# A Mamba scan whose column order is read across the rows of one input buffer

## The chip, the cores and the metric

The kernel runs on one core of a Trainium2 chip. The metric is device time in microseconds (us) of one execution of the whole program, from the first to the last instruction with a little around it; lower is better. All data are fp32.

## The reference

Eight images of 192 x 48 x 48 go through two layers. Layer 0 is a two-dimensional Mamba block (a selective scan in four directions), layer 1 an attention block with depthwise convolutions. The part that matters here is how layer 0 makes the four sequences of the scan and uses them:

```python
xx = gelu(depthwise_conv3x3(xx) + conv_b)               # (8, 384, 48, 48)
x_hw = xx.reshape(Bb, Dd, L)                            # by rows
x_wh = xx.transpose(0, 1, 3, 2).reshape(Bb, Dd, L)      # by columns
xs = jnp.stack([x_hw, x_wh, x_hw[..., ::-1], x_wh[..., ::-1]], axis=1)
x_dbl = jnp.einsum('bkdl,kcd->bkcl', xs, x_proj_w)      # x_proj: dts, B and C
dts, Bs_, Cs_ = jnp.split(x_dbl, [R, R + N], axis=2)
delta = softplus(einsum('bkrl,kdr->bkdl', dts, dt_w) + dt_b[None, :, :, None])
# per step: h = h * exp(delta * A) + (delta * u) * B ;  y = sum_n h * C
ys = selective_scan(xs, delta, A, Bs_, Cs_, Ds)         # K = 4 directions, N = 16 states
```

The four results are brought back to row order and added, then normalised, gated, projected (out_proj) and added to x.

## The kernel before

The 384 channels lie as J = 3 tiles of 128 partitions; a tile has L = 2304 positions (48 rows of 48), so one position is 4 bytes and one image row 192 bytes of a partition. A chunk is CH = 384 positions, 8 rows (or 8 columns), and a direction has NC = 6 chunks. Each of the eight images goes through four stages with a barrier of all engines after each: `front`, `scan_phase`, `back` and `attention`. Each engine runs its own program, ordered by hand, and semaphores hold them together. The convolution for the next image is done by the vector engine in the attention stage.

**The scan's input.** `u_v` holds the input twice: `u_v[:, 0]` by rows and `u_v[:, 1]` by columns. The convolution writes the row copy and ScalarE applies GELU to it in place, one channel tile at a time (L978, semaphore `gel`). The column copy is made in `front` by `column_copy`, one channel tile on each of three engines: VectorE tile 0 (L766), GpSimd tile 1 (L1206, a multiplication by one), ScalarE tile 2 (L980). Each of these reads with a stride of one image row and writes contiguously, waits for its tile's GELU, and counts up `uwh`.

**front on TensorE.** Two passes of x_proj (L463), o = 0 over the row copy after `gel` has reached 3, o = 1 over the column copy after `uwh` has reached 3. A pass has six groups, one for each chunk, of three matmuls 128x128 by 384 columns, accumulated over the channel tiles. The trace shows each fp32 matmul as two records, so a pass is 36 records and both are 72. A group goes to one of two PSUM banks of its pass; VectorE copies 64 rows of it into `stage` (L774) and ScalarE the other 64 into `dts` (L987). A bank may be filled again when both have read it. After a pass SyncE sends `stage[:, o]` to DRAM (L386), from where the rows of B and C are read back, broadcast over partitions, during the scan (L365).

**scan_phase.** Directions k = 0 to 3 one after the other, six chunks each; k even goes by rows, k odd by columns. For each chunk and each of the 16 states GpSimd multiplies `du` with a row of B (L1222), ScalarE makes exp(delta A) in PSUM (L1049), VectorE scans three times (L798), VectorE or GpSimd multiplies with C (L817 for ten states, L1232 for six), and TensorE adds the products in PSUM by an identity matmul (L490). Once a chunk:

- GpSimd makes `du` = delta times u for the next chunk (`delta_u`, L1211), between the work of states 12 and 13; the next L1222 needs it.
- ScalarE makes delta's softplus (L996 to L1007), VectorE its last step (L781), from matmuls of TensorE (L470).
- TensorE adds the y stored so far (L503, k = 1 to 3) or the skip term (L500, k = 0), and ScalarE stores y (L1031). y is kept by rows alone. So at k odd the three matmuls of L503 already read `y_v` in column order, eight columns of 48 positions with one image row (192 bytes) between neighbours, through the view `y_v.rearrange("p j (h w) -> p j w h", h=H)[..., 8 columns, :]`. At k = 2 the same line reads contiguous positions.

**Memory.** One buffer `area` is cut into parts by hand; the scan's parts lie behind `U`, one after the other.

Of the kernel before, what the change touches and what calls it, by code (L numbers as in the profile page):

```python
# [22 lines left out]
ALU = mybir.AluOpType  # L23
ACT = mybir.ActivationFunctionType
ds = bass.ds

NB, C, H, W = 8, 192, 48, 48
L = H * W
# [3 lines left out]
J = DI // 128  # L32
K, N, R = 4, 16, 12
CH = 8 * W
NC = L // CH
# [10 lines left out]


U = 0
DTS = U + 2 * J * L
DT0 = (64, 0, 96, 32)  # L50
ROWS = 4
ROWB = DTS + L
# [5 lines left out]
SCAN_END = HB + NH * JC  # L58
# [8 lines left out]
V = 0  # L67
XP2 = V + PAIRS * L
XN1 = XP2 + 3 * PADS
AREA = SCAN_END  # L70
X = AREA - CT * L
VT = X - MT * PAIRS * 128
KZ = VT - PAIRS * L
# [11 lines left out]
def build(nc, t, out):  # L85
    ctx = ExitStack()
    with ctx:
# [3 lines left out]
        def sem(name):  # L91
            return ctx.enter_context(nc.semaphore(name))
# [9 lines left out]
        d_diag = sb("d_diag", [128, J, 128])  # L102
        w_cv = sb("w_cv", [128, J, 9])
        b_cv = sb("b_cv", [128, J])
# [21 lines left out]
        ones = sb("ones", [128, 1])  # L126
# [17 lines left out]
        def ar(off, n, p0=0, p1=128):  # L144
            return area[p0:p1, off:off + n]

        u_v = ar(U, 2 * J * L).rearrange("p (o j l) -> p o j l", o=2, j=J)
        dts = ar(DTS, L)
        row_b = ar(ROWB, 2 * ROWS * CH).rearrange("p (s r l) -> p s r l", s=2, r=ROWS)
        row_c = ar(ROWC, 2 * ROWS * CH).rearrange("p (s r l) -> p s r l", s=2, r=ROWS)  # L150
# [42 lines left out]
        pad0 = sem("pad0")  # L193
        conv = sem("conv")
        gel = sem("gel")
        uwh = sem("uwh")
        xp_mm = sem("xp_mm")
        xp_ev = sem("xp_ev")
        xp_dv = sem("xp_dv")
# [63 lines left out]
        def alone(e):  # L263


            e.sem_inc(passed, 1)
# [11 lines left out]
        def wait_conv(e, b, j):  # L278

            e.wait_ge(conv, b * 54 + (18 * j + 18))  # L280
# [8 lines left out]
        def conv_taps(e, base, i, done, src, dst, w, bias):  # L289

            base = snap(e, base + 18 * i)
            acc = dst.rearrange("p (h w) -> p h w", h=H)
            for tap in range(9):
                dy, dx = divmod(tap, 3)
                for half in range(2):
                    r = H // 2 * half
                    a, x = acc[:, r:r + H // 2], src[:, r + dy:r + dy + H // 2, dx:dx + W]
                    if tap == 0:
                        e.tensor_scalar(a, x, w[:, i, 0:1], bias[:, i:i + 1], ALU.mult, ALU.add).then_inc(done, 1)  # L299
                    else:  # L300
                        e.wait_ge(done, base + (2 * tap - 1 + half))
                        e.scalar_tensor_tensor(out=a, in0=x, scalar=w[:, i, tap:tap + 1], in1=a,  # L302
                                               op0=ALU.mult, op1=ALU.add).then_inc(done, 1)
# [6 lines left out]
        def copy_vt(e, b, p, g):  # L310
# [2 lines left out]
            e.wait_ge(vt_mm, b * 10 + (5 * p + g + 1))  # L313
            e.activation(vt[:, p, 4 * g:min(4 * g + 4, MT)],
                         ps[:, 3 + g % 2, 0:n].rearrange("p (m c) -> p m c", c=128), ACT.Copy).then_inc(vt_ev, 1)

        def column_copy(e, b, j):

            wait_conv(e, b, J - 1)
            e.wait_ge(gel, b * 3 + (j + 1))  # L320
            return u_v[:, 1, j].rearrange("p (w h) -> p w h", w=W), u_v[:, 0, j].rearrange("p (h w) -> p w h", h=H)


        def walk(e, body):

# [9 lines left out]
        def pos(k, c):  # L335

            return c * CH if k < 2 else (NC - 1) * CH - c * CH
# [87 lines left out]
        def _(e):  # L425
# [27 lines left out]

            def front(b):
                for o in range(2):
                    e.wait_ge(gel if o == 0 else uwh, b * 3 + 3)
                    alone(e)
                    with e.Fori(0, 3) as cc:
                        for s in range(2):
                            e.wait_ge(xp_ev, b * 12 + cc * 2 + (6 * o + s + 1))  # L460
                            e.wait_ge(xp_dv, b * 12 + cc * 2 + (6 * o + s + 1))
                            for j in range(J):
                                m = e.matmul(ps[:, 2 * o + s, 0:CH], w_xp[:, j, o],  # L463
                                             u_v[:, o, j, ds(cc * 2 * CH + s * CH, CH)], start=j == 0, stop=j == J - 1)
                            m.then_inc(xp_mm, 1)

            def scan_phase(b):

                def delta_tile(k, c, j, bank=0):
                    e.matmul(ps[:, bank, 0:CH], w_dt[:, k, j * 128:(j + 1) * 128], dts[:, ds(pos(k, c), CH)],  # L470
                             start=True, stop=True).then_inc(dp_mm, 1)

                for j in range(J):
                    delta_tile(0, 0, j, 2 + j)

                def body(k, c, par, last, nxt):
                    g = e.snap(b * 24 + (c + k * NC))
                    g16, g3 = e.snap(g * 16), e.snap(g * 3)
                    gp, gd = e.snap(g * NP), e.snap(g * ND)
                    for i in range(N):  # L480
                        if i in POOL_N:
                            e.wait_ge(hcp, gp + (NP + POOL_N.index(i) + 1))
                            prod = hb[:, i % NH]
                        else:
                            e.wait_ge(hcs, gd + (1 + DVE_N.index(i) + 1))
                            prod = hc[:, DVE_N.index(i) % 2]
                        if i == 0:
                            e.wait_ge(yev, g + 1)
                        for j in range(J):
                            m = e.matmul(ps[:, 5 + j, 0:CH], ident[:], prod[:, j], start=i == 0, stop=i == N - 1)  # L490
                        m.then_inc(ysum, 1)
                        if nxt and i in (0, 2, 4):
                            e.wait_ge(dp_rd, g3 + (3 + i // 2))
                            if i == 0:
                                e.wait_ge(dp_v, g3 + 3)
                            delta_tile(*nxt, i // 2)
                        if i in (8, 10, 12):
                            j = (i - 8) // 2
                            if k == 0:
                                e.matmul(ps[:, 5 + j, 0:CH], d_diag[:, j], u_v[:, 0, j, ds(pos(k, c), CH)],  # L500
                                         start=False, stop=False)
                            else:
                                e.matmul(y_psum(k)[:, j], ident[:], y_chunk(k, c)[:, j], start=False, stop=False)  # L503

                walk(e, body)
# [194 lines left out]
        def _(e):  # L700
# [51 lines left out]
            def conv_tiles(b):  # L752
                e.wait_ge(pad0, b + 1)
                for j in range(J):
                    e.wait_ge(in_ev, b * 9 + (3 * j + 3))
                    conv_taps(e, b * 54, j, conv, xpad, u_v[:, 0, j], w_cv, b_cv)


            e.wait_ge(x_in, 16)
# [2 lines left out]
            conv_tiles(0)  # L762

            def front(b):
                o, u = column_copy(e, b, 0)
                e.tensor_copy(o, u).then_inc(uwh, 1)  # L766

                for o in range(2):
                    alone(e)
                    with e.Fori(0, 3) as cc:  # L770
                        for s in range(2):
                            m = e.snap(b * 12 + cc * 2 + (6 * o + s))
                            e.wait_ge(xp_mm, m + 1)
                            e.tensor_copy(stage[:, o, ds(cc * 2 * CH + s * CH, CH)],  # L774
                                          ps[0:4 * N, 2 * o + s, 0:CH]).then_inc(xp_dv, 1)
# [168 lines left out]
        def _(e):  # L944
# [28 lines left out]
            def front(b):  # L973
                alone(e)
                e.preload_act_table_set("gelu_and_others")
                for j in range(J):
                    wait_conv(e, b, j)
                    e.activation(u_v[:, 0, j], u_v[:, 0, j], ACT.Gelu).then_inc(gel, 1)  # L978
                o, u = column_copy(e, b, 2)
                e.activation(o, u, ACT.Copy).then_inc(uwh, 1)  # L980
                for o in range(2):
                    with e.Fori(0, 3) as cc:
                        for s in range(2):
                            q = 2 * o + s
                            at = cc * 2 * CH + s * CH
                            e.wait_ge(xp_mm, b * 12 + cc * 2 + (6 * o + s + 1))
                            e.activation(dts[64 - 64 * o:128 - 64 * o, ds(at, CH)], ps[64:128, q, 0:CH],  # L987
                                         ACT.Copy).then_inc(xp_ev, 1)
# [187 lines left out]
        def _(e):  # L1176
# [25 lines left out]
            next_conv(0)  # L1202

            def front(b):
                o, u = column_copy(e, b, 1)
                e.tensor_tensor(o, u, ones[:, 0:1, None].broadcast_to([128, W, H]), ALU.mult).then_inc(uwh, 1)  # L1206

            def scan_phase(b):
                def delta_u(g, par, k, c):
                    e.wait_ge(dp_v, g * 3 + 3)  # L1210
                    e.tensor_tensor(du[:, par], dlt[:, par], u_v[:, k % 2, :, ds(pos(k, c), CH)], ALU.mult)\  # L1211
                        .then_inc(dp_u, 1)

                g0 = e.snap(b * 24)
                delta_u(g0, 0, 0, 0)
# [146 lines left out]
```

## Time and profile before

| | |
|---|---|
| median of 3 runs | 16851.79 us (16836.97 to 16859.87) |
| the profiled execution's own time | 16839.18 us |
| its span, first to last instruction | 16837.4 us |
| mean granted TensorE clock | 0.927 |
| GpSimd busy | 11552.0 us (69%) |
| VectorE busy | 13601.2 us (81%) |
| TensorE busy | 12814.5 us (76%) |
| ScalarE busy | 10144.2 us (60%) |

An image takes about 2073 us. Busy shares over the whole span mix four stages that have different limits, so they say little about one edit; what an edit is worth is read in its own stage. Granted clock 1.0 is 2.4 GHz and 0.5 is 1.2 GHz, the only two levels seen.

### The profile page before, as it was taken

The page shows a single profiled execution, that of the slowest core. Times are in us where ns is not written, and L with a number is a line of the kernel's source. Part 1 is how long each engine was busy: PE and PEld are TensorE (multiplying, and loading weights), DVE is VectorE, ACT ScalarE, POOL GpSimd, SP SyncE. Part 2 cuts the span into 40 slices and gives each one's busy share as a digit, 9 for nine tenths or more (in the row PEclk, how much of TensorE's full clock was granted, in tenths as well). Part 3 has the DMA queues.
Part 4 walks back from the last instruction along what each step waited for, and adds up shares of the span by engine and source line. Part 5 has one row for each costly group of instructions (what it writes and reads, how often), then busy time and mean ns, then how long its engine had stood idle before and what let it go on. Part 6 is the DMA issues. An engine that isn't in the chain of part 4 may idle for free.

```text
span 16837.4 us, 196142 instructions
## 1 busy us (share of the span) xinstructions
PE 12814.5 (76%) x41612; PEld 6387.6 (38%) x41612; DVE 13601.2 (81%) x14280; ACT 10144.2 (60%) x19758; POOL 11552.0 (69%) x4604
## 2 busy tenths in 40 slices
PE   5777977779777797777977779677796777967779
PEld 2333433334333343333433334333343333433344
DVE  8998579985799857998579984899848998489984
ACT  4665556655566555665556655566556665566655
POOL 6997069970799707996079960899608996089950
PEclk8999999999899998999989999899998999999999
DMA  2332023320233202332023320233203332033310
GB/s 84 105 107 83 5 82 104 105 81 5 86 104 105 78 5 88 105 105 74 5 92 105 105 70 5 96 105 105 66 5 99 103 106 65 5 103 105 105 59 9
DMA packets 822115, 1276.86 MB, mean 76 GB/s; under 512 B 27488, under 2 KB 814560, under 8 KB 815136
## 3 DMA queue, kind: packets, MB, share of 16 engines
q1 hardware_dynamic: 820960, 1264.99, 23.6%
q14 instruction: 861, 7.05, 0.1%
q8 instruction: 294, 4.82, 0.1%
HBM read 1241.29 MB, written 23.59 MB: 75 GB/s over the span
## 4 chain that ended last, share of the span: by engine, by line
PE 29%; POOL 26%; issue 23%; DVE 18%; ACT 2%; DVEq 1%; POOLq 1%; ACTq 0%; SPq 0%; DMA 0%
POOL area L1222 18%; DVE area L798 13%; PE ps L654 8%; POOL area L1232 8%; PE ps L665 8%; PE ps L490 4%; DVE area L817 2%; PE ps L463 1%; DVE area L781 1%; PE ps L441 1%; PE ps L543 1%; PE ps L532 1%; DVE area L302 1%; PE ps L558 1%; POOL area L1211 1%
## 5 line engine op out<-in xcount | busy, mean ns | idle before, releaser
L490 PE MATMUL ps<-area,ident 128*128 128x384 f32 x18432 | 7317.3, 542 | 3436.6 <-POOL area L1232 1596.8
L798 DVE TENSOR_TENSOR_SCAN area<-ps,hst,area 128x384 f32<-128x384 f32 x9216 | 8617.5, 997 | 480.6 <-ACT ps L1049 419.2
L1222 POOL TENSOR_TENSOR area<-area 128x1152 f32<-128x1152 f32 x3072 | 7995.0, 2633 | 32.1 <-POOL area L1211 32.1
L1049 ACT ACTIVATE ps<-area,a_neg 128x384 f32<-128x384 f32 x9216 | 5236.8, 580 | 2485.2 <-DVE area L798 2464.1
L490 PEld LDWEIGHTS ps<-area,ident 128*128 128x128 f32 x18432 | 3626.1, 208 | 7243.4 <-POOL area L1232 2269.7
L1232 POOL TENSOR_TENSOR area<-area 128x1152 f32<-128x1152 f32 x1152 | 3027.9, 2628 | 102.4 <-ACT hst L1017 101.0
L817 DVE TENSOR_TENSOR area<-area,ps 128x1152 f32<-128x1152 f32 x1920 | 2550.2, 1328 | 5.2 <-ACT ps L1027 5.2
L1159 ACT ACTIVATE area<-ps,t_neg,area 128x768 f32<-128x768 f32 x1728 | 1617.7, 986 | 925.7 <-PE ps L654 925.7
L654 PE MATMUL ps<-area 64*128 64x384 f32 x6912 | 1370.3, 515 | 64.1 <-ACT area L1159 53.4
L1190 POOL TENSOR_TENSOR area<-w_in,ones 96x256 f32<-96x256 f32 x27 | 34.6, 1280 | 1992.1 <-DVE area L302 1353.5
L665 PE MATMUL ps<-area 128*64 128x384 f32 x6912 | 1341.6, 501 | 0.0
L1027 ACT ACTIVATE ps<-area 128x384 f32<-128x384 f32 x1920 | 922.4, 480 | 241.7 <-DVE area L817 240.7
L302 DVE SCALAR_TENSOR_TENSOR area<-area,w_dw 128x1152 f32<-128x1152 f32 x768 | 1024.8, 1411 | 0.0
L1184 POOL MEMSET area<- 128x50 f32 x33 | 5.1, 155 | 1476.1 <-PE ps L567 960.2
L654 PEld LDWEIGHTS ps<-area 64*128 64x128 f32 x6912 | 603.1, 188 | 808.9 <-ACT area L1159 504.8
L1206 POOL TENSOR_TENSOR area<-area,ones 128x2304 f32<-128x2304 f32 x8 | 44.2, 5526 | 1137.1 <-ACT area L978 1089.0
L665 PEld LDWEIGHTS ps<-area 128*64 128x64 f32 x6912 | 457.8, 136 | 786.5 <-issue 769.2
L1211 POOL TENSOR_TENSOR area<-area 128x1152 f32<-128x1152 f32 x192 | 505.7, 2634 | 253.5 <-DVE area L781 253.5
L299 DVE TENSOR_SCALAR area<-area,w_cv,b_cv 128x1152 f32<-128x1152 f32 x54 | 52.1, 1004 | 758.9 <-ACT area L962 758.9
L996 ACT ACTIVATE area<-ps,b_dt 128x384 f32<-128x384 f32 x576 | 330.2, 573 | 522.2 <-PE ps L470 520.6
L1031 ACT ACTIVATE area<-ps 128x1152 f32 (+1 forms) x192 | 312.2, 1626 | 514.5 <-PE ps L490 514.5
L302 DVE SCALAR_TENSOR_TENSOR area<-area,w_cv 128x1152 f32<-128x1152 f32 x432 | 576.4, 1408 | 0.0
(116 smaller groups left out, 8394.8 us busy)
## 6 DMA issues: line engine op xcount, KB each, us to landing
area<-bc_rows SPq DMA_DIRECT2D x1536, 768.0 KB, 6.4
area<-in_x SPq DMA_DIRECT2D x17, 1728.0 KB, 9.8
out<-area SPq DMA_DIRECT2D x8, 1728.0 KB, 9.1
bc_rows<-area SPq DMA_DIRECT2D x16, 576.0 KB, 4.7
w_dt<-in_w_dt SPq DMA_DIRECT2D x1, 768.0 KB, 6.5
w_in<-in_w_in SPq DMA_DIRECT2D x1, 576.0 KB, 4.6
w_qkv<-in_w_qkv SPq DMA_DIRECT2D x1, 576.0 KB, 5.4
w_xp<-in_w_xp SPq DMA_DIRECT2D x1, 384.0 KB, 4.9
```

Of the source, the lines that this page charges most:

```text
L302: e.scalar_tensor_tensor(out=a, in0=x, scalar=w[:, i, tap:tap + 1], in1=a, op0=ALU.mult, op1=ALU.add).then_inc(done, 1)
L490: m = e.matmul(ps[:, 5 + j, 0:CH], ident[:], prod[:, j], start=i == 0, stop=i == N - 1)
L654: i = e.matmul(ps[:, 2 * ((2 * m + h) % 3) + s, 0:CH], kz[rows, p, m * 128:(m + 1) * 128], q_v[rows, p, c * QC + s * CH:c * QC + (s + 1) * ...
L665: i = e.matmul(ps[64 * h:64 * h + 64, 6 + s, 0:CH], vt[:, p, m, 64 * h:64 * h + 64], pb[:, w % 4, s * CH:(s + 1) * CH], start=m == 0, stop ...
L798: e.tensor_tensor_scan(rev(hb[:, i % NH, j], k), rev(ps[:, 2 + j, 0:CH], k), rev(dbu[:, i % NH, j], k), hst[:, i, j:j + 1], ALU.mult, ALU. ...
L817: e.tensor_tensor(hc[:, d % 2], hb[:, i % NH], ps[:, 1:2, 0:CH].broadcast_to([128, J, CH]), ALU.mult).then_inc(hcs, 1)
L1027: e.activation(ps[:, 1, 0:CH], row_c[:, q % 2, i % ROWS], ACT.Copy).then_inc(c_ps, 1)
L1049: e.activation(ps[:, 2 + j, 0:CH], dlt[:, par, j], ACT.Exp, scale=a_neg[:, j, k, i:i + 1]).then_inc(da, 1)
L1159: e.activation(pb[:, w % 4].rearrange("p (s l) -> p s l", s=2), ps[:, 2 * (w % 3):2 * (w % 3) + 2, 0:CH], ACT.Exp, scale=ksc[:, p, w:w + 1 ...
L1211: e.tensor_tensor(du[:, par], dlt[:, par], u_v[:, k % 2, :, ds(pos(k, c), CH)], ALU.mult)\
L1222: e.tensor_tensor(dbu[:, i % NH], du[:, par], row_b[:, q % 2, i % ROWS:i % ROWS + 1].broadcast_to([128, J, CH]), ALU.mult).then_inc(dbus, 1)
L1232: e.tensor_tensor(hb[:, i % NH], hb[:, i % NH], row_c[:, q % 2, i % ROWS:i % ROWS + 1].broadcast_to([128, J, CH]), ALU.mult).then_inc(hcp, 1)
```

## The change

The column copy goes. `u_v` holds the input once, by rows, and `u_w` is a view of the same memory in column order. The three copying instructions per image and the semaphore `uwh` are gone (GpSimd has nothing left in `front` but its barrier). Two readers take the strided view instead: the matmuls of the second x_proj pass (18 for each image), and `delta_u` on GpSimd at k odd (12 of its 24 instructions for each image). The freed J * L positions are cut out behind `U`, so the scan's parts lie lower in `area`, whose total size stays.

```diff
-DTS = U + 2 * J * L
+DTS = U + J * L
...
-AREA = SCAN_END
+AREA = SCAN_END + J * L
...
-        u_v = ar(U, 2 * J * L).rearrange("p (o j l) -> p o j l", o=2, j=J)
+        u_v = ar(U, J * L).rearrange("p (j l) -> p j l", j=J)
+        u_w = u_v.rearrange("p j (h w) -> p j w h", h=H)
...
 TensorE, front:
-                    e.wait_ge(gel if o == 0 else uwh, b * 3 + 3)
+                    e.wait_ge(gel, b * 3 + 3)
...
                                 m = e.matmul(ps[:, 2 * o + s, 0:CH], w_xp[:, j, o],
-                                             u_v[:, o, j, ds(cc * 2 * CH + s * CH, CH)], start=j == 0, stop=j == J - 1)
+                                             (u_v[:, j, ds(cc * 2 * CH + s * CH, CH)], u_w[:, j, ds(cc * 16 + 8 * s, 8)])[o],
+                                             start=j == 0, stop=j == J - 1)
...
 VectorE, front:
-                o, u = column_copy(e, b, 0)
-                e.tensor_copy(o, u).then_inc(uwh, 1)
 ScalarE, front:
-                o, u = column_copy(e, b, 2)
-                e.activation(o, u, ACT.Copy).then_inc(uwh, 1)
 GpSimd, front:
-                o, u = column_copy(e, b, 1)
-                e.tensor_tensor(o, u, ones[:, 0:1, None].broadcast_to([128, W, H]), ALU.mult).then_inc(uwh, 1)
+                alone(e)
 GpSimd, scan_phase, delta_u:
-                    e.tensor_tensor(du[:, par], dlt[:, par], u_v[:, k % 2, :, ds(pos(k, c), CH)], ALU.mult)\
-                        .then_inc(dp_u, 1)
+                    if k % 2 == 0:
+                        e.tensor_tensor(du[:, par], dlt[:, par], u_v[:, :, ds(pos(k, c), CH)], ALU.mult).then_inc(dp_u, 1)
+                    else:
+                        e.tensor_tensor(du[:, par].rearrange("p j (w h) -> p j w h", w=8),
+                                        dlt[:, par].rearrange("p j (w h) -> p j w h", w=8),
+                                        u_w[:, :, ds(c * 8 if k < 2 else (NC - 1) * 8 - c * 8, 8)], ALU.mult).then_inc(dp_u, 1)
```

The other lines of the diff only drop the index 0 of `u_v[:, 0, ...]`.

## Rows read from the trace of the kernel before

**Rows 1.** Busy time by stage of one image: front, scan, back with attention.

```profile
core 0: us, PE busy (x) PEld busy (x) DVE busy (x) ACT busy (x) POOL busy (x), PEclk, DMA share, GB/s
2195.00:2234.00 39.00, 26.44 (x75) 14.98 (x74) 9.40 (x14) 17.78 (x18) 5.29 (x1) 0.82 0.22 64
2234.00:3745.00 1511.00, 1073.55 (x2730) 536.01 (x2729) 1415.60 (x1503) 981.31 (x2124) 1432.71 (x554) 0.93 0.32 102
3745.00:4268.00 523.00, 478.74 (x2328) 234.76 (x2328) 256.69 (x243) 267.33 (x328) 5.54 (x19) 0.94 0.02 4
```

**Rows 2.** Timeline of that front: start us, length us, engine, line, [idle before].

```profile
2200.23 6.15 ACT L978 ACTIVATE area<-area 128x2304 f32<-128x2304 f32 x3
2202.39 2.19 DVE L766 COPY area<-area 128x2304 f32<-128x2304 f32 x1 [6.24 <-ACT area L978]
2204.45 5.29 POOL L1206 TENSOR_TENSOR area<-area,ones 128x2304 f32<-128x2304 f32 x1 [153.97 <-ACT area L978]
2206.41 4.26 ACT L980 ACTIVATE area<-area 128x2304 f32<-128x2304 f32 x1
...
2207.07 25.65 PE L463 MATMUL ps<-area,w_xp 128*128 x72 [11.57 <-ACT area L978]
...
2211.41 0.48 ACT L987 ACTIVATE area<-ps 64x384 f32 x1 [0.74 <-PE ps L463]
...
2221.24 0.48 ACT L987 ACTIVATE area<-ps 64x384 f32 x1 [1.45 <-PE ps L463]
...
2223.18 0.49 ACT L987 ACTIVATE area<-ps 64x384 f32 x1 [1.45 <-PE ps L463]
```

**Rows 3.** The chain that ended last, the same front: start us, us, what.

```profile
2200.23 6.16 ACT area L978 x3
2206.39 0.68 issue
2207.07 25.67 PE ps L463 x72
```

**Rows 4.** L503 between its neighbours on TensorE, at k = 1 and at k = 2.

```profile
2705.03 1.45 PE L503 MATMUL ps<-area,ident 128*128 x2
2706.30 2.11 PE L490 MATMUL ps<-area,ident 128*128 128x384 f32 x6
...
3131.42 0.81 PE L503 MATMUL ps<-area,ident 128*128 x2
```

**Rows 5.** Single lines: count, shortest/median/longest in ns.

```profile
L503 PE MATMUL ps<-area,ident x864: 486/804/823, 561.1 to 16228.2; 128*128 x115, 128*128 128x384 f32 x58
L463 PE MATMUL ps<-area,w_xp x576: 486/486/1004, 123.3 to 14782.2; 128*128 x192
L978 ACT ACTIVATE area<-area x24: 2105/2110/2128, 98.8 to 14753.4; 128x2304 f32<-128x2304 f32 x24
L980 ACT ACTIVATE area<-area x8: 4203/4276/4334, 122.6 to 14755.6; 128x2304 f32<-128x2304 f32 x8
```

**Rows 6.** The same view of GpSimd's lines.

```profile
L1206 POOL TENSOR_TENSOR area<-area,ones x8: 5268/5281/7227, 120.6 to 14753.6; 128x2304 f32<-128x2304 f32 x8
L1211 POOL TENSOR_TENSOR area<-area x192: 2608/2631/2693, 158.3 to 16165.7; 128x1152 f32<-128x1152 f32 x192
L1190 POOL TENSOR_TENSOR area<-w_in,ones x27: 608/609/2877, 17.2 to 16682.8; 96x256 f32<-96x256 f32 x27
```

**Rows 7.** Busy time by direction, chunk starts to chunk starts: k = 0, 1, 2, 3.

```profile
2298.24:2596.29 298.05, 209.65 (x540) 106.58 (x540) 289.83 (x307) 197.67 (x437) 297.14 (x117) 0.93 0.32 106
2717.20:3024.17 306.97, 221.82 (x541) 108.74 (x540) 289.28 (x306) 201.48 (x436) 297.71 (x116) 0.92 0.32 103
3083.82:3383.31 299.49, 211.99 (x540) 106.33 (x540) 288.97 (x306) 197.17 (x436) 297.61 (x116) 0.93 0.33 106
3383.31:3622.97 239.66, 167.86 (x433) 81.75 (x432) 232.12 (x246) 161.92 (x350) 238.19 (x93) 0.96 0.33 106
```

**Rows 8.** Busy time by part of the front: first group of L463, then the rest.

```profile
2207.00:2211.50 4.50, 4.43 (x7) 2.52 (x8) 0.06 (x1) 3.76 (x2) 2.73 (x1) 0.50 0.00 0
2211.50:2222.00 10.50, 10.50 (x34) 6.16 (x33) 3.23 (x6) 2.82 (x6) 0.00 (x0) 1.00 0.01 2
2222.00:2233.00 11.00, 10.72 (x34) 6.00 (x32) 2.88 (x6) 2.58 (x6) 0.00 (x0) 1.00 0.25 54
```

More of the change, by code:

```diff
@@ L195, in build @@
         gel = sem("gel")
-        uwh = sem("uwh")
         xp_mm = sem("xp_mm")
@@ L315, in copy_vt @@
                          ps[:, 3 + g % 2, 0:n].rearrange("p (m c) -> p m c", c=128), ACT.Copy).then_inc(vt_ev, 1)
[L317 to L321, printed above, removed]
         def walk(e, body):
@@ L499, in body @@
                             if k == 0:
-                                e.matmul(ps[:, 5 + j, 0:CH], d_diag[:, j], u_v[:, 0, j, ds(pos(k, c), CH)],
+                                e.matmul(ps[:, 5 + j, 0:CH], d_diag[:, j], u_v[:, j, ds(pos(k, c), CH)],
                                          start=False, stop=False)
@@ L755, in conv_tiles @@
                     e.wait_ge(in_ev, b * 9 + (3 * j + 3))
-                    conv_taps(e, b * 54, j, conv, xpad, u_v[:, 0, j], w_cv, b_cv)
+                    conv_taps(e, b * 54, j, conv, xpad, u_v[:, j], w_cv, b_cv)
             e.wait_ge(x_in, 16)
@@ L977, in front @@
                     wait_conv(e, b, j)
-                    e.activation(u_v[:, 0, j], u_v[:, 0, j], ACT.Gelu).then_inc(gel, 1)
-                o, u = column_copy(e, b, 2)
-                e.activation(o, u, ACT.Copy).then_inc(uwh, 1)
+                    e.activation(u_v[:, j], u_v[:, j], ACT.Gelu).then_inc(gel, 1)
                 for o in range(2):
```

## The prediction

> **What bounds the kernel now.** I began with busy time cut by stage, because the page's shares mix stages. The change touches two of them: the front, 39 us of an image's 2073, and the scan, 1511 us [rows 1]. The reader is to see in that view that no engine fills the front (TensorE 26.44 of 39 us, GpSimd 5.29, VectorE 9.40), while in the scan GpSimd is busy for 1432.71 of 1511 us and VectorE for 1415.60.
>
> For the front I then read the chain that ended last: three GELUs of ScalarE, 6.16 us, an issue of 0.68, and 25.67 us of x_proj matmuls without a break [rows 3]. None of the three column copies is in it. The timeline says why. x_proj's first pass needs the row copy alone; it starts 0.66 us behind the last GELU, and the copies run under it. VectorE's ends at 2202.39 + 2.19 = 2204.58, GpSimd's at 2204.45 + 5.29 = 2209.74 and ScalarE's at 2206.41 + 4.26 = 2210.67 [rows 2]. The second pass, which needs them, begins when the first has ended, near 2221: the eviction at 2221.24 is the sixth and the last of pass 0 [rows 2]. The copies are ready some 10 us early.
>
> For the scan I cut the busy time by direction. In k = 0 and k = 2 GpSimd works without a gap (297.14 of 298.05 us, 297.61 of 299.49), in k = 3 nearly so (238.19 of 239.66 for four chunks), and only in k = 1 does it stand still, 306.97 - 297.71 = 9.26 us over five chunks, 1.85 us a chunk [rows 7]. So a longer instruction on GpSimd is paid at once, except in k = 1.
>
> **The change, part by part.**
>
> *Removed: three copies and the wait on* `uwh`. They take 2.19, 5.29 and 4.26 us of three engines for each image [rows 2]. What hides them is the first x_proj pass. Could one of them still hold something up? Only ScalarE's has a successor nearby, the first eviction of x_proj. The copy ends at 2210.67 and the eviction starts at 2211.41, after 0.74 us of waiting for the matmuls [rows 2]. It isn't late, and the second bank gives the matmuls another group of room. So I take a gain of 0. Were that cover gone, the copies would cost at most the longest, 5.29 us for each image or 42 us in all; that is the far end and nothing in the chain points to it.
>
> *Changed: the second x_proj pass reads across the rows.* The trace of before has this very access. L503 at k odd reads y in column order, eight columns of 48 positions, with one image row between neighbours, for 384 columns of output; at k = 2 it is the same instruction with contiguous input. Two records, which are one fp32 matmul, take 0.81 us at k = 2 and 1.45 us at k = 1 [rows 4]. A record's own length there is 0.486 or 0.804 us [rows 5], so the second record starts 0.81 - 0.486 = 0.32 us behind the first when contiguous and 1.45 - 0.804 = 0.65 us when strided. The next instruction confirms it: at k = 1 it starts 2706.30 - 2705.03 = 1.27 us after the pair's start [rows 4], 0.64 us for each record. In the front today a group of three matmuls, six records, takes 2223.18 - 2221.24 = 1.94 us, 0.32 us a record [rows 2]. So each matmul of pass 1 goes from 0.64 to 1.28 us.
>
> Does the doubling belong to the stride or to a crowded memory in the scan? ScalarE answers that. In the quiet front it reads the same buffer with the same stride in L980 at 4276 ns, and 2304 contiguous elements in L978 at 2110 ns [rows 5], although the two functions differ. I take the full doubling. The pass has 18 matmuls: 18 x 0.64 = 11.5 us for each image.
>
> Does it lie on the path? The chain is TensorE alone from 2207.07 to the end of the front [rows 3]; evictions of 0.48 us wait for each group [rows 2] and now will wait longer. Nothing covers it. Behind the pass stand the last eviction, the barrier, and all that follows it, so all of it is paid: 8 x 11.5 = **92 us**. The second transfer of `stage` to DRAM goes out 11.5 us later with the barrier and keeps its distance to its readers; the first isn't moved.
>
> *Changed:* `delta_u` *at k odd reads across the rows on GpSimd.* 12 x 8 = 96 instructions. Behind each on the same engine stands the next product with B, and behind that VectorE's scan. Here no row has the same thing, so bounds. GpSimd's column copy reads with exactly this stride, beside a constant as its second input: 5281 ns for 2304 elements, 2.29 ns each [rows 6]. `delta_u` with two contiguous inputs takes 2631 for 1152, 2.28 ns each [rows 6]. Is the constant perhaps cheap and hides a price? L1190 has a contiguous input and the same constant: 609 ns for 256, 2.38 ns each with its fixed part [rows 6], no cheaper. So the stride costs GpSimd nothing that these rows can show; 5281/2 - 2631 = 10 ns. The lower end is 0 (a stride that makes it faster has no reason). The upper end is a doubling as on ScalarE, +2.63 us. I take 10 ns, since L1206 is the same engine, operation and stride: 96 x 0.01 = **1 us**.
>
> The Trainium skill speaks against this value. GPSIMD Engine Reference, section Performance pitfalls for Q7 kernels, says that a read with a step over 8 bytes costs about 2.9 instead of 1.9 cycles for each element, half as much again. Here the step is 192 bytes, and L1206 doesn't show it, though with one strided stream beside a constant. By that page the sum would be the one of the rival "GpSimd pays", below, instead of 93 us.
>
> *Moved: the scan's parts lie J x L positions lower.* No operand changes its shape or partition, no transfer its size: 0, within what the runs scatter.
>
> *Sum:* 0 + 92 + 1 = +93 us, on the profiled execution's own 16839.18 us 16932 us. The median of the runs shown, 16851.79, lies 12.6 us above that execution; on it the sum gives **16945 us**, +0.55%.
>
> **The rivals.**
>
> *GpSimd pays for the stride.* One of two inputs doubles its share: 2.63/2 = 1.31 us more for each `delta_u`. The `du` for a chunk is made in the chunk before, so of 12 instructions for each image seven fall where GpSimd has no gap (the last chunk of k = 0, the last of k = 2, five in k = 3), and five in k = 1, where 1.85 us a chunk stand free [rows 7] and swallow 1.31. 7 x 1.31 x 8 = 73 us more, 17018 us in all. With the upper end of 2.63 us: 7 x 2.63 + 5 x (2.63 - 1.85) = 22.3, times 8, 178 us more, 17123 us. For it: no row has one strided and one contiguous input. Against: L1206 and L1190.
>
> *The granted clock falls in the slower pass.* Today it is 0.50 in the first group and 1.00 in the rest of the front [rows 8]. If the strided pass ran at 0.5 and its reads slowed in step, a matmul would take 2.56 us: 18 x 1.28 x 8 = 184 us more, 17129 us. For it: the strided L503 has no record longer than 823 ns, so none at the low level is to be seen [rows 5], and its price there is unknown. Against: TensorE has no gap in the pass, and the first group, with 0.64 us a record at clock 0.50, was what preceded the rise to 1.00 [rows 8].
>
> *No slower: the stride is free in the front.* If the doubling of L503 came from other engines' reads in the scan, pass 1 would stay at 1.94 us a group: 16853 us, within 0.2%. Between the two, each 0.1 us off the strided matmul's extra 0.64 is worth 18 x 0.1 x 8 = 14 us, so it decides this below an extra of (34 - 1)/144 = 0.23 us. Against: the median of 864 records is 804 and the longest 823 [rows 5], which is no scatter of contention, and ScalarE's copy doubled in the quiet front.
>
> **How the numbers follow.** Forecast 0.78, GpSimd pays 0.10, clock falls 0.06, stride free 0.04, and 0.02 for a gain that I don't see (the copies had held something up, and the pass is also free). A change within 0.2% (34 us) can't be told from none here. The forecast's own range is 16925 to 16970: the pair's 1.27 to 1.30 us, clock of the first matmuls, and the scatter of the runs (23 us from lowest to highest). To leave out no more than 2 in 10 with some room for an unknown size, the range goes up to the first rival: 16925 to 17025. Faster 0.02, within 0.2% 0.04, slower 0.94.
>
> **What would show it.** In the profile of the changed kernel: x_proj's matmuls still 576 records, half of them near 804 ns; evictions of the second pass 3.85 us apart instead of 1.94; the front 50 us instead of 39; no wait for L980's like, and the chain of the front TensorE throughout. L1211's successor in two forms of equal length, about 2.63 us, chunks in k = 0, 2 and 3 still 59.6 to 60 us apart. The prediction is wrong if the strided form on GpSimd is longer by over 0.3 us (7 x 0.3 x 8 = 17 us), if the strided pass shows clock 0.50, or if its groups come less than 3 us apart.

## The result, and the profile after

The changed kernel takes 16956.59 us (median of 6 runs, 16952.94 to 16960.43) against 16852.44 us for the kernel before (6 runs, 16836.97 to 16859.87). The ratio is 1.0061, with a 95% interval of 1.005 to 1.0072: 104 us slower, where 93 us were forecast. The profiled execution took 16956.64 us with a span of 16954.8 us, 117.4 us above the span of before; before's profiled execution was 13 us quicker than its median.

The line numbers moved: x_proj is L456, its evictions L976 (ScalarE) and L765 (VectorE), GELU L969, `delta_u` L1200 (k even) and L1202 (k odd), the product with B L1214.

Busy time by stage of the same image, to be laid beside [rows 1]:

```profile
core 0: us, PE busy (x) PEld busy (x) DVE busy (x) ACT busy (x) POOL busy (x), PEclk, DMA share, GB/s
2212.00:2263.00 51.00, 38.33 (x75) 15.57 (x73) 7.21 (x13) 13.27 (x16) 0.00 (x0) 0.87 0.17 49
2263.00:3775.00 1512.00, 1076.83 (x2714) 537.96 (x2715) 1414.01 (x1499) 980.35 (x2120) 1439.23 (x554) 0.92 0.32 102
3775.00:4299.00 524.00, 482.78 (x2325) 234.69 (x2324) 257.90 (x245) 269.71 (x332) 5.60 (x19) 0.94 0.02 4
```

The front has grown from 39 to 51 us, and TensorE's busy time in it from 26.44 to 38.33. GpSimd has nothing left in it. In the scan GpSimd is busy for 6.5 us more. The chain that ended last, in that front, beside [rows 3]:

```profile
2217.22 6.16 ACT area L969 x3
2223.38 0.68 issue
2224.06 37.95 PE ps L456 x72
```

The same three links; only the matmuls grew, 37.95 - 25.67 = 12.3 us. The timeline (start us, length us, [idle before]) shows which:

```profile
2228.40 0.49 ACT L976 ACTIVATE area<-ps 64x384 f32 x1 [5.03 <-PE ps L456]
2231.18 0.49 ACT L976 ACTIVATE area<-ps 64x384 f32 x1 [2.30 <-PE ps L456]
2233.12 0.49 ACT L976 ACTIVATE area<-ps 64x384 f32 x1 [1.45 <-PE ps L456]
...
2238.92 0.49 ACT L976 ACTIVATE area<-ps 64x384 f32 x1 [1.45 <-PE ps L456]
...
2242.79 0.49 ACT L976 ACTIVATE area<-ps 64x384 f32 x1 [3.38 <-PE ps L456]
2246.66 0.49 ACT L976 ACTIVATE area<-ps 64x384 f32 x1 [3.38 <-PE ps L456]
...
2262.13 0.49 ACT L976 ACTIVATE area<-ps 64x384 f32 x1 [3.38 <-PE ps L456]
```

A group of the first pass still takes 1.94 us; one of the second takes 3.87, six times. That is (3.87 - 1.94) x 6 = 11.6 us for each image. The other 0.7 us of this image's 12.3 lie in the second group of the first pass, 2.78 us (2231.18 - 2228.40) instead of 2.10, at a mean granted clock of 0.74 instead of 0.98. Over the eight images the first pass isn't longer: from its first record to that of the second pass it is 13.7 us, and 14.2 before (means). The granted clock was not the cause of the 11.6 us: in the second pass it reads 1.00, 2.4 GHz, while TensorE is busy without a gap.

```profile
2240.00:2261.00 21.00, 21.00 (x34) 6.70 (x33) 2.75 (x5) 2.44 (x5) 0.00 (x0) 1.00 0.13 28
```

Single lines, shortest/median/longest in ns, beside [rows 5, 6]:

```profile
L456 PE MATMUL ps<-area,w_xp x576: 486/821/1004, 122.2 to 14887.9; 128*128 x192
L1202 POOL TENSOR_TENSOR area<-area x96: 3173/3204/3272, 523.5 to 16283.0; 128x1152 f32<-128x1152 f32 x96
L1200 POOL TENSOR_TENSOR area<-area x96: 2607/2630/2690, 168.3 to 15917.4; 128x1152 f32<-128x1152 f32 x96
```

This is where the forecast was off. `delta_u` with the strided input takes 3204 ns, 574 more than with a contiguous one, where 10 were forecast. Busy time by direction, beside [rows 7], k = 0 to 3:

```profile
2327.53:2626.79 299.26, 210.82 (x540) 106.60 (x540) 287.82 (x304) 196.36 (x433) 297.24 (x116) 0.93 0.33 106
2686.95:2991.45 304.50, 217.79 (x540) 106.62 (x540) 289.80 (x306) 201.86 (x436) 300.30 (x117) 0.93 0.32 104
3052.83:3352.23 299.40, 210.45 (x541) 106.14 (x540) 289.07 (x306) 197.56 (x436) 297.53 (x117) 0.93 0.32 106
3352.23:3594.86 242.63, 174.44 (x433) 85.41 (x432) 231.56 (x245) 160.66 (x349) 240.41 (x94) 0.92 0.33 104
```

In k = 3 GpSimd's busy time and the time of the chunks both rise, 2.2 and 3.0 us in four chunks. In k = 1 GpSimd is busy for 300.30 instead of 297.71 us, yet the five chunks are *shorter*, 304.50 instead of 306.97. There the longer instruction cost nothing; something else had set the pace.

The whole account, from the starts of the 192 `delta_u` in GpSimd's timelines of the two profiled executions: from an image's last to the next image's first it is 720.8 us after and 709.6 before (means of seven), +11.2. Within the scan, first to last, it is 1383.6 and 1380.0 (means of eight), +3.6. 8 x (11.2 + 3.6) = 118 us, about the 117.4 us of the two spans.

### The profile page after: what moved, and what is told of

It reads as the page before. It is cut to its first block, busy times and chain, and to the rows that moved or that the text cites. A ratio compares the mean times of both kernels' runs of the same rounds, so it can differ in the third digit from the quotient of the medians.

```text
span 16954.8 us, 196086 instructions
## 1 busy us (share of the span) xinstructions
PE 12921.5 (76%) x41612; PEld 6398.5 (38%) x41612; DVE 13590.9 (80%) x14272; ACT 10116.2 (60%) x19750; POOL 11560.1 (68%) x4596
## 4 chain that ended last, share of the span: by engine, by line
POOL 31%; PE 29%; issue 26%; DVE 11%; ACT 2%; POOLq 1%; DVEq 1%; ACTq 0%; SPq 0%; DMA 0%
POOL area L1214 20%; POOL area L1224 9%; PE ps L648 8%; PE ps L659 8%; DVE area L789 8%; PE ps L484 4%; PE ps L456 2%; POOL area L1202 2%; DVE area L808 1%; PE ps L434 1%; PE ps L537 1%; PE ps L526 1%; DVE area L302 1%; DVE area L772 1%; PE ps L552 1%
## 5 line engine op out<-in xcount | busy, mean ns | idle before, releaser
L1214 POOL TENSOR_TENSOR area<-area 128x1152 f32<-128x1152 f32 x3072 | 7994.1, 2634 | 32.1 <-POOL area L1200 16.0
L1224 POOL TENSOR_TENSOR area<-area 128x1152 f32<-128x1152 f32 x1152 | 3028.9, 2629 | 84.8 <-ACT hst L1006 82.9
L1200 POOL TENSOR_TENSOR area<-area 128x1152 f32<-128x1152 f32 x96 | 252.9, 2635 | 1518.9 <-DVE area L772 1518.9
L497 PE MATMUL ps<-area,ident 128*128 (+1 forms) x864 | 533.5, 704 | 0.0
```

Source lines behind the costliest of these rows:

```text
L1214: e.tensor_tensor(dbu[:, i % NH], du[:, par], row_b[:, q % 2, i % ROWS:i % ROWS + 1].broadcast_to([128, J, CH]), ALU.mult).then_inc(dbus, 1)
L1224: e.tensor_tensor(hb[:, i % NH], hb[:, i % NH], row_c[:, q % 2, i % ROWS:i % ROWS + 1].broadcast_to([128, J, CH]), ALU.mult).then_inc(hcp, 1)
```

## The experiments

**1. One part at a time.** In `pe_alone` the copies stay and only x_proj's second pass reads across the rows:

```diff
-                    e.wait_ge(gel if o == 0 else uwh, b * 3 + 3)
+                    e.wait_ge(gel, b * 3 + 3)
...
-                                             u_v[:, o, j, ds(cc * 2 * CH + s * CH, CH)], start=j == 0, stop=j == J - 1)
+                                             (u_v[:, 0, j, ds(cc * 2 * CH + s * CH, CH)], u_w[:, j, ds(cc * 16 + 8 * s, 8)])[o],
+                                             start=j == 0, stop=j == J - 1)
```

> The column copy and its three instructions stay and the scan reads it; only the second x_proj pass reads the row copy with a stride. Theory A (the pass is paid in full and the copies were hidden): +90 to +92 us on the kernel before, groups of the second pass 3.86 us apart, GpSimd's delta_u at 2.63 us. Rival B (part of the 104 us comes from the lost copies or the moved memory, not from the matmuls): clearly below 85 us. Rival C (the strided matmuls cost more than 92 because they also slow what follows): over 100 us.

Measured: 16945.75 us against 16858.37, ratio 1.0053 (1.004 to 1.0067), +87 us. The evictions of the second pass:

```profile
2240.97 0.49 ACT L989 ACTIVATE area<-ps 64x384 f32 x1 [1.45 <-PE ps L464]
2244.83 0.49 ACT L989 ACTIVATE area<-ps 64x384 f32 x1 [3.38 <-PE ps L464]
2248.70 0.49 ACT L989 ACTIVATE area<-ps 64x384 f32 x1 [3.38 <-PE ps L464]
```

3.87 us a group, as in the changed kernel. 87 us lies between A's 90 and B's 85, and the interval (+67 to +113 us) can't tell them apart. The trace does: from an image's last `delta_u` to the next image's first it is 721.2 us here and 709.6 before (means of seven), 11.6 us more, or 93 in eight images. Experiment 2 measures the same term from the other side.

In `pool_alone` the copies stay too, x_proj reads them, and only `delta_u` at k odd is as in the change.

> The column copy stays and x_proj reads it; only delta_u at k odd reads the row copy with a stride on GpSimd. Each of its 96 instructions takes 0.57 us more, 55 us together. Theory A (seven of twelve lie where GpSimd has no gap): 7 x 0.57 x 8 = +32 us. Rival B (the scan changes between two paces and gives most of it back): +5 to +20 us, with chunks of k = 1 nearer to 60.3 than to 61.4 us. Rival C (all is paid): +55 us.

Measured: 16861.67 us, ratio 1.0002 (0.9993 to 1.0011), +3 us (-12 to +19). The instruction is as long as in the changed kernel (3203 ns), 55 us in all; little of it arrives, and Theory A's 32 us lie outside the interval. Rival B, or even less. Its busy time at k = 1 and k = 3:

```profile
2664.49:2967.29 302.80, 217.31 (x540) 106.25 (x540) 289.69 (x306) 202.09 (x436) 300.17 (x117) 0.93 0.32 105
...
3328.09:3571.05 242.96, 171.68 (x433) 83.64 (x432) 231.51 (x245) 160.58 (x349) 240.51 (x93) 0.94 0.33 104
```

302.80 instead of 306.97 us in k = 1, and 242.96 instead of 239.66 in k = 3 [rows 7]: in this image given back in one direction, paid in the other. The other images differ. Over all eight the scan, first to last `delta_u`, is 1383.7 us instead of 1380.0, and the two spans differ by 25 us. But the profiled execution of before is 19 us quicker than the median of this comparison (16839.18 against 16858.37), so that the small sum rests on the medians and not on this pair of traces.

`no_copy` is the changed kernel with both strided reads replaced by contiguous ones (`u_v[:, j, ds(...)]` for both passes, `u_v[:, :, ds(pos(k, c), CH)]` for every k), so only the loss of the copies and the new places in memory remain.

> The changed kernel with the two strided reads replaced by contiguous reads of the row copy (the second x_proj pass and delta_u at k odd then work on positions in row order, so directions 1 and 3 are computed on other data). What is left of the change is the lost copies and the moved memory. Theory A: 0 within 10 us, the front 39 us long. Rival B (the copies did hold something up): -10 to -42 us. Rival C (the new places in memory slow an access): over +10 us, with one of the scan's instructions longer than before.

Measured: 16838.62 us, ratio 0.9987 (0.9978 to 0.9996), -20 us. A failed. The number lies in B's range, but the trace doesn't show B's mechanism: the front's 72 records take 25.63 us, as before [rows 2, 3], so the copies held nothing up there. The profiled execution happened to be the longest, 16881.56 us, with 1386.3 us for the scan against 1380.0 before, so where the others save isn't in a trace.

`filler` is no_copy with a product on GpSimd in front of each `delta_u` at k odd:

```diff
+                    if k % 2:
+                        e.tensor_tensor(ar(SCAN_END, 240), w_dt[:, 0, 0:240], w_dt[:, 1, 0:240], ALU.mult)
                     e.tensor_tensor(du[:, par], dlt[:, par], u_v[:, :, ds(pos(k, c), CH)], ALU.mult).then_inc(dp_u, 1)
```

> As no_copy, and in front of each delta_u at k odd GpSimd does one more product of 240 elements on a part of memory that nothing else uses, about 0.57 us, as long as the stride costs. Directions 1 and 3 are again computed on other data. Theory A (only the length on GpSimd counts): the same above no_copy as pool_alone above the kernel before, within 8 us. Rival B (the strided reads also disturb VectorE or ScalarE): filler is cheaper by over 10 us and VectorE's scan is longer in pool_alone.

Measured: 16865.57 us, ratio 1.0004 (0.9995 to 1.0014): +7 us on the kernel before, and +27 us on no_copy, its own base. The filler came out at 702 ns, somewhat longer than the stride's 574. It is not cheaper than the stride, and VectorE's scan is as long in both (994 ns on average): rival B is out. Theory A failed too: it wanted the filler to cost the same above no_copy, within 8 us, as the stride costs above the kernel before, and about the same work costs 3 us on one base and 27 on the other. In the same image the filler's k = 1 takes 305.58 us in five chunks and isn't shortened as in pool_alone. Why the base matters stays open.

**2. The pass without its price.** `runs8` is the changed kernel, but the second pass reads, from each image row, the chunk's eight columns together. The result lies in PSUM by (row, column), and the two evictions, which wait for each group anyway, put it into column order:

```diff
-  (u_v[:, j, ds(cc * 2 * CH + s * CH, CH)], u_w[:, j, ds(cc * 16 + 8 * s, 8)])[o],
+  (u_v[:, j, ds(cc * 2 * CH + s * CH, CH)], u_v[:, j].rearrange("p (h w) -> p h w", h=H)[:, :, ds(cc * 16 + 8 * s, 8)])[o],
...
+  to, got = stage[:, o, ds(...)], ps[0:4 * N, 2 * o + s, 0:CH]
+  if o:
+      to, got = to.rearrange("p (w h) -> p w h", w=8), got.rearrange("p (h w) -> p w h", w=8)
+  e.tensor_copy(to, got).then_inc(xp_dv, 1)
```

> The changed kernel with the second x_proj pass reading each image row's eight columns together, runs of 8 adjacent elements (32 bytes) instead of single ones; the chunk then lies in PSUM in the order (row, column), and VectorE's and ScalarE's evictions, which have over a microsecond to spare for each group, put it into column order. Theory A (the price hangs on how far the next element is, and is paid for single elements only): groups of the second pass 1.94 us apart again, front 39 us, +3 to +15 us on the kernel before, as pool_alone. Rival B (every strided pattern runs at half rate): 3.86 us a group and +100 us. Rival C (the evictions become the bound): over 2.2 us a group, evictions over 1.1 us each.

Measured: 16861.87 us against 16853.03, ratio 1.0006 (0.9997 to 1.0015), +9 us. Its x_proj line, and two evictions of the second pass:

```profile
L456 PE MATMUL ps<-area,w_xp x576: 485/486/1004, 122.3 to 14784.2; 128*128 x192
```
```profile
2229.88 0.49 ACT L981 ACTIVATE area<-ps 64x384 f32 x1 [1.45 <-PE ps L456]
2231.81 0.49 ACT L981 ACTIVATE area<-ps 64x384 f32 x1 [1.45 <-PE ps L456]
```

1.93 us a group, and the eviction that reads PSUM with a stride of 32 bytes still takes 0.49 us. Theory A holds. Against the changed kernel this is 104 - 9 = 95 us less, each compared with its own runs of the kernel before; the forecast had 92 for the pass.

**3. What the price hangs on.** Three kernels, run once each, differ from the changed one only in which elements the strided reads take. `stride2` and `stride4` take every second and fourth element (`u_v.rearrange("p j (l s) -> p j s l", s=2)[:, j, 0, 0:CH]`), `short_runs` eight runs of 48 adjacent elements (`"p j (h s w) -> p j s h w", s=2, w=W`).

> The changed kernel, but the strided reads are replaced by eight runs of 48 adjacent elements with a gap of one row between runs (the data of directions 1 and 3 are then others). It asks whether GpSimd's 0.57 us is the price of the stride or of an access pattern in short pieces. Theory A (the stride): delta_u at k odd 2.63 us, matmul records 0.486 us. Rival B (pieces): delta_u 3.2 us.

> The changed kernel, but the strided reads take every second element, 8 bytes apart (the data of directions 1 and 3 are then others). Theory A (the price comes with the distance of 192 bytes, several elements still share one fetch here): delta_u at k odd 2.63 us and matmul records of the second pass 0.486 us. Rival B (any stride but one costs): 3.2 us and 0.82 us. In between: GpSimd free and TensorE not, or the other way round.

> As stride2 with every fourth element, 16 bytes apart (the data of directions 1 and 3 are then others). Theory A (the price comes when neighbours are 16 bytes or more apart, whatever the distance): matmul records of the second pass 0.80 to 0.82 us and delta_u at k odd 3.2 us, the same as at 192 bytes. Rival B (it grows with the distance): 0.50 to 0.75 us and 2.7 to 3.1 us.

Their `delta_u` at k odd, in the order short_runs, stride2, stride4:

```profile
L1203 POOL TENSOR_TENSOR area<-area x96: 2613/2632/2672, 511.9 to 16194.3; 128x1152 f32<-128x1152 f32 x96
```
```profile
L1203 POOL TENSOR_TENSOR area<-area x96: 2657/2675/2770, 513.7 to 16179.9; 128x1152 f32<-128x1152 f32 x96
```
```profile
L1203 POOL TENSOR_TENSOR area<-area x96: 3197/3238/3296, 527.0 to 16292.6; 128x1152 f32<-128x1152 f32 x96
```

And two evictions of the second pass of stride2, then of stride4:

```profile
2238.12 0.49 ACT L977 ACTIVATE area<-ps 64x384 f32 x1 [1.55 <-PE ps L457]
2240.16 0.49 ACT L977 ACTIVATE area<-ps 64x384 f32 x1 [1.55 <-PE ps L457]
```
```profile
2254.57 0.49 ACT L977 ACTIVATE area<-ps 64x384 f32 x1 [3.58 <-PE ps L457]
2258.62 0.49 ACT L977 ACTIVATE area<-ps 64x384 f32 x1 [3.57 <-PE ps L457]
```

| neighbours apart | TensorE, us a group (mean) | GpSimd, ns (median) |
|---|---|---|
| 4 bytes, runs of 48 | 1.94 | 2632 |
| 8 bytes | 2.04 | 2675 |
| 16 bytes | 4.06 | 3238 |
| 192 bytes | 3.87 | 3204 |

Theory A holds in all three, apart from 5% at 8 bytes for TensorE and 2% for GpSimd: a step between 8 and 16 bytes, and no growth with the distance. The times of single executions were 16867.78, 16855.92 and 16969.49 us, the last with the slow pass, like the changed kernel's. The Trainium skill (SBUF — State Buffer, the note on SBUF cachelines in the section Door 1: The DMA port swizzle) says that a 16-byte line wants at least two hits for full bandwidth; stride2 has two on a line and stride4 one, and the trace agrees, but for the 5%. The same note puts the free stride at 4 fp32; stride4 took just that step and paid, so there the measurement decides.

**4. Where GpSimd's 55 us go.** In k = 1 something other than GpSimd had set 61.4 us a chunk. ScalarE's timeline of before shows it waiting twice within one chunk:

```profile
2735.03 2.13 ACT L1031 ACTIVATE area<-ps 128x1152 f32 x1 [3.08 <-PE ps L490]
2736.95 1.58 ACT L1049 ACTIVATE ps<-area,a_neg 128x384 f32<-128x384 f32 x3
...
2741.73 0.58 ACT L996 ACTIVATE area<-ps,b_dt 128x384 f32<-128x384 f32 x1 [2.70 <-PE ps L470]
```

First 3.08 us for the last chunk's y, then 2.70 us for the first delta tile, which TensorE makes behind products that themselves wait for that y to be stored. VectorE needs the exponentials that ScalarE makes in between, and stands still at both places:

```profile
2737.58 2.83 DVE L798 TENSOR_TENSOR_SCAN area<-ps,hst,area 128x384 f32<-128x384 f32 x3 [2.38 <-ACT ps L1049]
2742.82 2.83 DVE L798 TENSOR_TENSOR_SCAN area<-ps,hst,area 128x384 f32<-128x384 f32 x3 [1.16 <-ACT ps L1049]
```

The edit of `delta_first`, on the kernel before, moves that tile to the front of TensorE's work for the chunk:

```diff
                     for i in range(N):
+                        if nxt and i == 0:
+                            e.wait_ge(dp_rd, g3 + 3)
+                            e.wait_ge(dp_v, g3 + 3)
+                            delta_tile(*nxt, 0)
...
-                        if nxt and i in (0, 2, 4):
+                        if nxt and i in (2, 4):
                             e.wait_ge(dp_rd, g3 + (3 + i // 2))
-                            if i == 0:
-                                e.wait_ge(dp_v, g3 + 3)
```

> The kernel before, with one thing moved: TensorE makes the first delta tile of the next chunk in front of the products of state 0, which wait until y has been stored, instead of behind them; ScalarE then no longer waits 1.1 to 2.7 us for it right behind that store. Theory A (the chunks of 61.4 us hang on ScalarE's two waits, of which this takes one): k = 1 goes to 59.6 to 60.5 us a chunk, -20 to -60 us. Rival B (only the wait for y counts): within 12 us. Rival C (VectorE's slack is used up elsewhere and GpSimd falls behind): slower by over 12 us.

Measured: 16764.08 us against 16872.19, ratio 0.9935 (0.9922 to 0.9949), -108 us, more than Theory A gave. Part of it is the comparison's: the kernel before was at 16872 us in that one and at 16852 to 16858 in the others, against which it would be 88 to 94 us. The two profiled executions differ by 75 us in span, 68 of them in the scan (8 x (1380.0 - 1371.5)). So the sign and the mechanism are shown, the size lies between 75 and 108. Busy time at k = 1 and k = 3:

```profile
2652.51:2951.31 298.80, 217.83 (x541) 104.76 (x540) 288.89 (x306) 202.73 (x436) 297.49 (x117) 0.94 0.33 106
...
3309.36:3549.33 239.97, 171.97 (x432) 83.44 (x432) 230.56 (x244) 160.88 (x348) 238.24 (x93) 0.94 0.34 106
```

k = 1 now runs at GpSimd's pace, 298.80 us with 297.49 busy, 59.8 us a chunk. ScalarE's waits over the whole kernel, before and in delta_first (us in total, times, longest):

```profile
ACT area L996 <- PE ps L470: 520.6, 322, 4.7
```
```profile
ACT area L998 <- PE ps L470: 267.6, 153, 4.6
```

If GpSimd is now the pace, a longer instruction on it has nowhere to hide. `runs8_delta_first` has runs8's reads (the strided `delta_u` among them) and this edit.

> runs8 (no column copy, second x_proj pass in runs of eight, delta_u strided on GpSimd) with the first delta tile moved as in delta_first. If delta_first reaches GpSimd's pace, then GpSimd's 0.57 us has nowhere to hide and this kernel is 25 to 55 us above delta_first (Theory A). Rival B (the 0.57 us is still absorbed): within 12 us of delta_first.

Measured: 16816.25 us, ratio 0.9967 (0.9955 to 0.998): 52 us above delta_first on the same chip, of the 96 x 0.574 = 55 us that the instruction is longer. Its k = 1:

```profile
2658.96:2960.56 301.60, 218.69 (x540) 106.19 (x540) 289.08 (x306) 202.87 (x436) 300.24 (x117) 0.93 0.33 105
```

301.60 - 298.80 = 2.8 us in five chunks, 0.56 us each, as much as the instruction is longer. The kernel also lacks the copies, but k = 0 and k = 2, where `delta_u` is contiguous, take the same in both (298.09 and 298.05 us, 298.33 and 298.39), and k = 3 takes 241.52 instead of 239.97. Theory A holds.

Two kernels tried the other wait, with the store of y moved behind state 3 (`if i == 3 and last:` in place of `i == 2`), on the kernel before (`store3`) and with the moved tile (`delta_first3`).

> The kernel before, with one thing moved: ScalarE stores the last chunk's y behind state 3 of the new chunk instead of state 2. Theory A (chunks of 61.4 us come from ScalarE standing 3 to 3.5 us before that store while VectorE waits for its exponentials, so with the store later GpSimd's 59.6 us is the pace everywhere): chunks 59.6 to 59.8 us in all directions, -40 to -75 us. Rival B (the pace is set elsewhere, or the wait only moves): within 12 us of the kernel before. Rival C (TensorE's products start too late and stall VectorE through the buffers of h): slower by over 20 us.

> delta_first with the store of y behind state 3 instead of state 2, as in store3. Theory A (store3 lost its time in the wait for the first delta tile, 4.48 us a chunk): at least 200 of the 342 us that store3 cost are gone. Rival B (the late store itself stalls the scan): within 60 us of store3, 17195 us.

store3 took 17195.61 us, ratio 1.0202 (1.0188 to 1.0215), +343 us: Rival C by its size, but its reason, the buffers of h, is not what the trace shows. delta_first3 took 16795.05 us, ratio 0.9955 (0.9942 to 0.9969). The total waits of VectorE for the exponentials in the kernel before, of ScalarE for delta tiles and of VectorE for the exponentials in store3, and the same two of delta_first3:

```profile
DVE area L798 <- ACT ps L1049: 419.2, 293, 2.9
```
```profile
ACT area L996 <- PE ps L470: 860.9, 204, 5.6
DVE area L798 <- ACT ps L1049: 788.2, 189, 5.9
```
```profile
ACT area L998 <- PE ps L470: 739.4, 320, 5.4
DVE area L800 <- ACT ps L1051: 187.7, 189, 2.9
```

In store3 the first tile came later still, and VectorE stood 788 us for the exponentials queued behind it, 369 more than before, about what the kernel lost. With the first tile made early, ScalarE still waits nearly as long for the later tiles, but VectorE's wait shrinks to 188 us and the kernel is 400 us quicker than store3: Theory A of delta_first3 holds. It is no gain over delta_first.

## Why the prediction came out right, and where it didn't

The forecast of 16945 us missed the measured 16956.59 by 12 us, and its largest term was right in mechanism and size. That the total came this close is in part luck: one term was off by 54 us of GpSimd's time, and the scan absorbed most of it.

**The second pass, +92 us.** Right, in mechanism and size. L503 had the same access in the trace of before, and the price that its pairs showed, 1.28 for 0.64 us a matmul, is the one measured (3.87/3 = 1.29). Nothing covered it, since the chain of the front was this engine alone. Alone it measured +87 (11.6 us an image in the trace, 93 in all), and taken out of the changed kernel -95.

**The copies, 0 us.** The cover was read rightly: in no_copy the front is no shorter. But no_copy as a whole is 20 us quicker than the kernel before, with the interval clear of none. The gap from one image's scan to the next is nearly the same (708.8 against 709.6 us), so it probably comes from the scan's pace, which differs between images even in one execution (k = 1 takes 357.8 us for six chunks in the first and last image of before and 366.5 in the others). That is argued and not shown: whether the freed instructions or the new places in memory tip it, no run separates.

**delta_u, +1 us.** This step failed, by its size: the instruction costs 0.574 us more, not 0.01. The prediction had named "longer by over 0.3 us" as a sign of being wrong, and that sign came. The row chosen for it, GpSimd's column copy, has a constant beside the strided stream, where `delta_u` has a second contiguous one. It also runs in the front, and `delta_u` in the scan with VectorE at work. Which of the two makes the difference between [rows 6] and L1202 isn't shown; no run has two streams and a stride outside the scan. The Trainium skill's rule (GPSIMD Engine Reference, section Performance pitfalls for Q7 kernels) had the sign and the threshold right, its half as much again came out as 22% here, 3204 for 2631 ns. It deserved more than a chance of 0.10.

**What that cost.** The rival "GpSimd pays" would, by its own sum, have made 7 x 0.574 x 8 = 32 us of it. The kernel paid 3 (pool_alone), 9 (runs8, which has the lost copies too) or, with the pace set free by delta_first, 52. So the step was mis-sized, and its place was too simple: the prediction had the slack of k = 1 as a fixed 1.85 us a chunk. There the chunks were paced by a round of waits through TensorE, ScalarE and VectorE, and in pool_alone that round was even shorter, 60.6 instead of 61.4 us a chunk in the image shown. How a longer instruction on GpSimd shortens it is not shown.

**The clock and the free stride.** Both rivals are out: granted clock 1.00 in the strided pass, and a full doubling in the quiet front.

**The sum of the parts.** Measured one at a time on the kernel before, the pass, `delta_u` and the lost copies give 87 + 3 - 20 = 70 us, not 104. With the filler's 27 in place of the 3 they give 94. Each of the three has an interval of 15 to 23 us either way, and the scan's pace depends on what else is changed, so the pass is settled to some 10 us, and how the rest of the 104 divides is not.

## What to carry to other kernels

Before a copy that only reorders data is dropped, look whether it lay in the chain at all, and what its readers will pay: here three copies hidden under matmuls were exchanged for 11.6 us an image on the engine that was the chain. If the copy has to go, let the reader take short runs of adjacent elements and reorder in an eviction that waits anyway; that cost 9 us in place of 104. And where a pace is longer than every engine's busy time, as in k = 1 here, look for a round of waits: on the kernel before it swallowed most of a small cost, and one reordered instruction that broke it was worth 75 to 108 us, about as much as the change under study.

## What the runs showed of the hardware that wasn't expected

- TensorE and GpSimd both pay for a strided fp32 read between a step of 8 and one of 16 bytes: 2.04 against 4.06 us for a group of three matmuls by 384 columns, 2675 against 3238 ns for a product of 128x1152. At 192 bytes it is a little less than at 16, 3.87 us and 3204 ns.
- GpSimd's product takes 2.28 ns an element with two contiguous inputs, 2.29 with a strided one and a constant (5281 ns for 2304), and 2.78 with a strided and a contiguous one (3204 for 1152). The middle one was measured in the front, the other two in the scan.
- Runs of eight adjacent elements (32 bytes) from rows 192 bytes apart cost TensorE nothing, 485 to 486 ns a record, and ScalarE evicts 64x384 from PSUM with a stride of 32 bytes in the same 0.49 us.
